# Graph layers with folded sums in three bf16 parts, and early expert rows: one kernel on one Trainium2 core

## The chip, the cores and the metric

The kernel runs on one core of one Trainium2 chip. The metric is the device time of one execution in microseconds (us); the median over the runs is what is compared.

## What is computed

The reference is a block of three parts over N = 3125 tokens of width D = 256 in fp32.

```
h = layernorm(x)                                   # no gain
ew = clip(|edge_weight|, 1e-6); deg = segment_sum(ew, dst) + 1; dis = 1/sqrt(deg)
for W, b, g, be in two layers:                     # 50,000 edges src -> dst, dst sorted
    xw = h @ W
    agg = segment_sum(dis[src]*ew*dis[dst] * xw[src], dst) + dis^2 * xw + b
    h = relu(layernorm(agg)*g + be) + h
x = x + h
# mixture of 16 experts, each token to its 2 best
n = layernorm(x); logits = n @ gate_w + gate_b; top 2, softmax of the two
y = n + sum_k w_k * (relu(n @ w1[e_k] + b1[e_k]) @ w2[e_k] + b2[e_k])
out = x + layernorm(y)*gamma + beta
```

The gate's bias has a spread of 0.388, the logits' own spread is 16 * 0.02 = 0.32. So the experts are loaded unevenly. Computed from the reference's own inputs, the 16 experts get 115, 28, 2028, 135, 1120, 1083, 7, 4, 57, 50, 8, 341, 741, 0, 532 and 1 of the 6250 assignments. Of the 18 token tiles that the kernel seats first (the tokens from 896 up), experts 0 to 3 get 87, 14, 1436 and 102.

## The kernel before, in words

Tokens lie in NT = 25 tiles of 128. A graph layer is a dense product: the edge weights are laid out as a matrix in DRAM (`weights_by_cell`), whose rows are not tokens but 128 x VT = 26 "virtual tiles" (v = dst + number of the block of 256 edges), so that rows which two blocks of edges write don't meet. The products of a virtual tile are its raw sums; a second small product, the fold, adds the raw rows of virtual tiles t, t+1 and t+2 that belong to a token tile.

Four stretches follow each other in time.

1. **Edges to matrix.** 196 blocks of 256 edges (`s`), in 98 pairs (`p`). For a pair a compare makes a 0/1 matrix of equal (src, dst) keys, on VectorE (`compare`, L656) or, for the 28 pairs of `ACT_PAIRS`, on ScalarE (`act_compare`, L907: four Abs, L916, and a Relu, L921); TensorE sums the equal edges' weights with it (`weigh`, L1074, in bf16). GpSimd then scatters the cells with 391 indirect DMAs (`place`, L474), chunk of 4 blocks by chunk, into the matrix that SyncE blanked tile by tile (L366). Beside it run the degrees, the first layernorm, and the tables h @ W1. GpSimd starts when `limits_ready` (VectorE's `limits_back`) says how many chunks each tile waits for. Constants come from GpSimd iotas (L437 to L459); `limits` waits for all 14 (`LATE_CONSTS`).
2. **Layer 1**, steps k = 0 to 25 of the loop at L1210 on, and
3. **Layer 2**, steps k = 26 to 51, tiles in falling order. In step k TensorE makes the raw sums of one virtual tile: 25 fp32 products of 128x128 by 128x256 (L1238), from a ring of three matrix tiles that SyncE loads (L386; in layer 1 each load first waits for the scatter's semaphores `seconds`, L381). Inside the step, after 4 of the 25 (`s == 4`), it folds the raw sums of step k-1 (`combine`, L1182): at most three products of `fold` (0/1, made by VectorE in `folding`, L756 and L759) by `ov`, ScalarE's fp32 copy of the raw sums (`take_out`, L962). The same step also turns a tile (L1096 or L1190) and makes its product or its gate logits (L1107, L1198). VectorE finishes the folded tile (`finish_tile`, L764 to L800: degree scale, bias, layernorm, relu, residual; ScalarE makes its NaN marks and roots, L966 to L975), and in layer 2 also finds slots for an earlier tile (`seat`, L827 to L832) and chooses the experts of another (`choose`, L807 to L821). GpSimd writes each seated tile's token numbers to their slots in DRAM (L522, `homes_in`). Between its ring loads SyncE issues the experts' weights: `load_up` (L142) and `load_down` (L147), 512 KB each. The last 17 of them stand at its end, after the waits for the steps that free their room.
4. **Experts.** The graph part is one block of the program and the experts' part the next; between them all five engines meet at a barrier, SyncE's issues included. Then VectorE makes the table of expert blocks (L1538 to L1557, 60 entries), SyncE loads the rows of slots (`load_ids`, L1377; the first `FIXED` = 4 blocks of 128 rows belong to experts 0 to 3 and need no table, but all slots written), GpSimd gathers the tokens of a block (`fetch`, L1333), and TensorE turns and multiplies them (L1401, L1418, L1430), block after block, 58 in the usual case. A last block (L1644 on) adds the two experts' rows of each token and normalises.

The fold and the order around it, which the change touches:

```
def combine(k):
    pe.wait_ge(fold_ready, k + 1)
    pe.wait_ge(ov_ready, k + 1)
...
for s in range(NT):
    if s == 4:
        combine(k - 1)
```

## Time and profile before

| what | value |
|---|---|
| median of 3 runs | 1240.26 us (1239.3 to 1245.99) |
| profiled execution, own time | 1235.6 us |
| its span | 1234.1 us |
| TensorE busy | 1095.5 us, 89% |
| VectorE busy | 708.5 us, 57% |
| GpSimd busy | 594.1 us, 48% |
| ScalarE busy | 386.6 us, 31% |

The span runs from the first to the last instruction. Edges to matrix take it to 259 us, layer 1 to 585 us, layer 2 to 935 us, the experts from 966 to 1195 us, the last block the rest. In rows of the trace a time is where an instruction starts, then how long it takes; an fp32 product shows as two MATMUL records. In brackets stands how long the engine sat idle before it, and whose result ended that.

### The profile page before, as it was taken

The page shows a single profiled execution, that of the slowest core. Times are in us where ns is not written, and L with a number is a line of the kernel's source. Part 1 is how long each engine was busy: PE and PEld are TensorE (multiplying, and loading weights), DVE is VectorE, ACT ScalarE, POOL GpSimd, SP SyncE. Part 2 cuts the span into 40 slices and gives each one's busy share as a digit, 9 for nine tenths or more (in the row PEclk, how much of TensorE's full clock was granted, in tenths as well). Part 3 has the DMA queues.
Part 4 walks back from the last instruction along what each step waited for, and adds up shares of the span by engine and source line. Part 5 has one row for each costly group of instructions (what it writes and reads, how often), then busy time and mean ns, then how long its engine had stood idle before and what let it go on. Part 6 is the DMA issues. An engine that isn't in the chain of part 4 may idle for free. (4 is left out here: it accounts for less than half of the span.)

```text
span 1234.1 us, 19478 instructions
## 1 busy us (share of the span) xinstructions
PE 1095.5 (89%) x6441; PEld 956.5 (78%) x6444; DVE 708.5 (57%) x2025; ACT 386.6 (31%) x879; POOL 594.1 (48%) x625
## 2 busy tenths in 40 slices
PE   2687687699999999999799999999993699999966
PEld 1566565588888888888588888888882699999955
DVE  8999743543434434434347777777777354555437
ACT  0578545831111111111111111111111133333357
POOL 4777777777777777750001111111112355555525
PEclk9999887999999999999799999999997799999989
DMA  7999540033433433430145535445447422222237
GB/s 283 294 392 385 221 161 2 2 114 107 149 119 107 151 117 107 150 118 1 51 150 188 207 129 194 163 147 181 145 168 248 130 74 70 74 71 74 69 100 248
DMA packets 79728, 180.76 MB, mean 146 GB/s; under 512 B 28994, under 2 KB 58316, under 8 KB 73228
## 3 DMA queue, kind: packets, MB, share of 16 engines
q1 hardware_dynamic: 48360, 151.67, 34.3%
q0 software_dynamic: 19776, 15.76, 4.8%
q10 hardware_dynamic: 11492, 12.07, 3.0%
q8 instruction: 54, 0.88, 0.3%
q14 instruction: 46, 0.38, 0.1%
HBM read 122.12 MB, written 57.33 MB: 145 GB/s over the span
## 5 line engine op out<-in xcount | busy, mean ns | idle before, releaser
L474 POOL DMA_INDIRECT weights_by_cell<-w_cell,cell x391 | 399.7, 1022 | 132.8 <-issue 118.0
L1238 PE MATMUL ps<-w 128*128 128x256 f32 x1300 | 300.7, 384 | 1.1 <-ACT w L904 1.1
L1238 PE MATMUL ps<-x_rows,w 128*128 128x256 f32 x1250 | 281.4, 379 | 0.3 <-DVE w_cell L662 0.3
L1238 PEld LDWEIGHTS ps<-w 128*128 128x128 f32 x1300 | 243.0, 191 | 33.0 <-ACT w L904 2.6
L1238 PEld LDWEIGHTS ps<-x_rows,w 128*128 128x128 f32 x1250 | 235.7, 190 | 31.5 <-DVE w_cell L662 0.4
L522 POOL DMA_INDIRECT token_and_home_of_slot<-pair,slot_id x50 | 49.6, 992 | 353.2 <-DVE slot_id L832 345.6
L1567 DVE TENSOR_SCALAR hidt<-ps,b1t 128x128 f32<-128x128 f32 x232 | 65.3, 344 | 90.9 <-PE ps L1418 90.9
L1430 PE MATMUL ps<-w,hidt 128*128 (+1 forms) x464 | 109.8, 379 | 0.0
L1418 PEld LDWEIGHTS ps<-xt,w1s 128*128 128x128 f32 x880 | 106.9, 192 | 2.8
L1046 PE MATMUL ps<-key_part,pick 128*128 128x256 f16 x196 | 50.4, 353 | 65.8 <-DVE layer L656 36.0
L1418 PE MATMUL ps<-xt,w1s 128*128 128x128 f32 x880 | 107.1, 275 | 0.0
L656 DVE TENSOR_TENSOR layer<-ps,w 128x1024 bf16<-128x1024 f32 x70 | 84.9, 1219 | 31.1 <-PE ps L1046 30.3
L1339 POOL DMA_INDIRECT expert_rows_by_token<-yb,ids x58 | 57.0, 983 | 91.4 <-DVE yb L1582 91.1
L1430 PEld LDWEIGHTS ps<-w,hidt 128*128 128x128 f32 x464 | 83.6, 190 | 9.0
L773 DVE COPY_PREDICATED layer<-mark,zeros 128x256 f32<-128x256 int32 x50 | 22.5, 450 | 108.2 <-ACT mark L966 108.2
L1046 PEld LDWEIGHTS ps<-key_part,pick 128*128 128x128 f16 x196 | 15.9, 112 | 80.2 <-DVE layer L656 38.7
L1333 POOL DMA_INDIRECT xb<-normalised_rows,ids x60 | 58.6, 976 | 31.3 <-PE ps L1401 16.0
L1182 PE MATMUL ps<-layer 128*128 128x256 f32 x296 | 72.4, 379 | 0.3 <-ACT layer L962 0.3
L764 DVE TENSOR_TENSOR layer<-ps,x_rows 128x256 f32<-128x256 f32 x25 | 10.6, 426 | 102.1 <-PE ps L1182 102.1
L1492 ACT ACTIVATE xt<-ps 128x256 f32<-128x256 f32 x60 | 23.0, 383 | 144.7 <-PE ps L1401 144.7
L1107 PE MATMUL ps<-wmat,ht 128*128 128x256 f32 x200 | 61.3, 435 | 5.8 <-ACT ht L895 5.6
L1081 PE MATMUL ps<-w,hot 128*128 128x75 bf16 x400 | 64.8, 319 | 0.0
(242 smaller groups left out, 1470.0 us busy)
## 6 DMA issues: line engine op xcount, KB each, us to landing
w<-weights_by_cell SPq DMA_DIRECT2D x49, 1600.0 KB, 7.2
weights_by_cell<-w SPq DMA_DIRECT2D x26, 1600.0 KB, 8.7
w<-in_L_ffn_w_dram SPq DMA_DIRECT2D x32, 512.0 KB, 8.6
weights_by_cell<-w_cell,cell POOLq DMA_INDIRECT x391
w<-in_x_dram ACTq DMA_DIRECT2D x1, 3072.0 KB
hot<-in_x_dram ACTq DMA_DIRECT2D x24, 128.0 KB, 2.1
normalised_rows<-hot ACTq DMA_DIRECT2D x24, 128.0 KB, 4.8
out_dram<-w SPq DMA_DIRECT2D x24, 128.0 KB
```

The costliest lines, as they stand in the source:

```text
L474: pool.indirect_dma_start(adj[:, :], bass.IndirectOffsetOnAxis(ap=cell[0:m, c:c + 1].bitcast(U32), axis=0), w_cell[0:m, n, half * CH + j:h ...
L656: dve.tensor_tensor(same[:, d % MRING, :, :, :], bank(d % KBANKS).rearrange("p (s h q) -> p s h q", s=2, h=1).to_broadcast(wide), own.rear ...
L1046: mm = pe.matmul(bank(at, k * SBE, (k + 1) * SBE), pick[:, j:j + 1].to_broadcast([P, P]), key_part[:, g, :], start=True, stop=True)
L1081: mm = pe.matmul(bank(6, 0, 3 * NT), hot[:, i % DRING, :, k], hot_w[:, i % DRING, :, :, k].rearrange("p a b -> p (a b)"), start=(i == 0 an ...
L1107: mm = pe.matmul(bank(6 if q else 3, 0, D), ht[:, i % 2, c, :], wmat[:, q, c, :], start=(c == 0), stop=(c == KD - 1))
L1182: mm = pe.matmul(bank(2 + i % 3, 0, D), fold[:, k % 2, (d - lo) * P:(d - lo + 1) * P], ov[:, k % 2, :], start=begins, stop=ends)
L1238: mm = pe.matmul(bank(k % 2, 0, D), ring[:, place_of(k), s * P:(s + 1) * P], tab[q][:, s, :], start=(s == 0), stop=(s == NT - 1))
L1333: pool.indirect_dma_start(xb[:, b % ring, :], None, x2_dram[0:N, :], bass.IndirectOffsetOnAxis(ap=ids[:, b % IDS, 0:1].bitcast(U32), axis= ...
L1339: pool.indirect_dma_start(planes[:, :], bass.IndirectOffsetOnAxis(ap=ids[:, b % IDS, 1:2].bitcast(U32), axis=0), yb[:, b % 2, :], None).th ...
L1418: mm = pe.matmul(ph[s][:, f * P:(f + 1) * P], w, xt[:, s, c, :], start=(c == 0), stop=(c == KD - 1))
L1430: mm = pe.matmul(py[s], hidt[:, s, c, :], w, start=(c == 0), stop=(c == KF - 1))
L1567: ins = dve.tensor_scalar(hidt[:, s, c, :], ph[s][:, c * P:(c + 1) * P], bias, 0.0, ALU.add, ALU.max)
```

## The change

- **Fold in bf16, both layers** (`SPLIT_LAYERS` = 2). The raw sums are cut in three bf16 parts whose sum is exact: ScalarE copies the high part, VectorE subtracts it from the sums (`split`), ScalarE copies the middle part of the rest, VectorE subtracts again. `combine` makes three bf16 products per tile with a bf16 `fold` where it made one in fp32. It stands after 7 of the 25 products of the step instead of 4.
- **First expert rows.** In SyncE's queue, before the wait for step 50 and the 17 last weight loads, stand now: a wait for `need_ready`, which VectorE's `seat(18)` sets, a wait for the slots of the first 18 tiles (`homes_first`), a wait for `homes_in` up to a number held in a register, and the four loads of `ids`. The number is 16 (one more scatter), plus 208 if the smallest count of experts 0 to 3 over the first 18 tiles is under 128; 224 is all of the other 7 tiles. The rows b1 are loaded in the first stretch by SyncE.
- **ScalarE compares ahead.** `act_compare` of the next pair of `ACT_PAIRS` stands after ScalarE's work of the pair before, no more right ahead of its use.
- **Small ones.** `limits` waits for 8 constants; the big iotas are cut in pieces of 256 or 512 elements; x is loaded after the first blank and the other blanks after x; the table of empty slots (`unplaced`) has room of its own, so ScalarE no longer waits for its store (L936 before); a few semaphores are merged.

```diff
+SEATED = 18
+PARTS, SPLIT_LAYERS = 3, 2
...
                         sp.wait_ge(blanked[t % 2], 16 * (t // 2 + t % 2))
+                    if t == 1:
+                        sp.wait_ge(x_in, 32)
                     if t == 3:
...
+                        sp.dma_start(b1r[TURN * KF:EXPERTS * KF, :],
+                                     g["eb1"][0:EXPERTS - TURN].rearrange("e (c p) -> (e c) p", p=P)).then_inc(b_in, 16)
+                        sp.dma_start(b1r[0:TURN * KF, :],
+                                     g["eb1"][EXPERTS - TURN:EXPERTS].rearrange("e (c p) -> (e c) p", p=P)).then_inc(b_in, 16)
...
                 sp.wait_ge(ov_ps, 2 * VT - 2)
                 for e in (3, 4):
                     load_up(sp, e)
+                later = sp.alloc_register("later_need")
+                sp.wait_ge(need_ready, 1)
+                sp.reg_load(later, later_need[0:1, 0:1])
+                sp.wait_ge(homes_first, 32 * SEATED)
+                sp.wait_ge(homes_in, sp.snap(later, min_val=16, max_val=32 * (NT - SEATED)))
+                for b in range(FIXED):
+                    sp.dma_start(ids[:, b, :], home[b * REGION:b * REGION + P, :]).then_inc(ids_in[b], 16)
                 sp.wait_ge(ov_ps, 2 * VT - 1)
                 for e in range(3):
...
-                pool.iota(low, pattern=[[1, NT * P + 1]], base=0, channel_multiplier=0,
-                          allow_small_or_imprecise_dtypes=True).then_inc(late_consts, 1)
+                for k in range(0, NT * P + 1, 512):
+                    pool.iota(low[:, k:min(k + 512, NT * P + 1)], pattern=[[1, min(512, NT * P + 1 - k)]], base=k, channel_multiplier=0,
+                              allow_small_or_imprecise_dtypes=True).then_inc(late_consts, 1)
...
                             home[:, :], bass.IndirectOffsetOnAxis(ap=slot_id[0:m, k, d:d + 1].bitcast(U32), axis=0),
-                            pair[0:m, k, d, :], None).then_inc(homes_in, 16)
+                            pair[0:m, k, d, :], None).then_inc(homes_first if r < SEATED else homes_in, 16)
...
-                    dve.wait_ge(late_consts, LATE_CONSTS)
+                    dve.wait_ge(late_consts, LIMIT_CONSTS)
...
+                    dve.tensor_tensor((fold_bits if in_parts(k) else fold)[:, k % 2, 0:w], reach[:, 0:w], reach[:, 1:w + 1], ALU.subtract).then_inc(fold_ready, 1)
+
+                def split(k):
+
+                    dve.wait_ge(ov_high, k + 1)
+                    dve.tensor_tensor(ov_rest, ov_bank(k), ov_parts[:, k % 2, 0, :], ALU.subtract).then_inc(ov_left, 1)
+                    dve.wait_ge(ov_left, k + 1)
+                    dve.wait_ge(ov_mid, k + 1)
+                    dve.tensor_tensor(ov_parts[:, k % 2, 2, :], ov_rest, ov_parts[:, k % 2, 1, :], ALU.subtract).then_inc(ov_ready, 1)
 
...
+                    if r == SEATED:
+                        link(dve.tensor_copy(rank0[:, :], bank(5, 0, FIXED)))
                     dve.tensor_tensor(rank[:, :], bank(5, 0, EXPERTS), base[:, :], ALU.add).then_inc(rank_read, 1)
                     dve.wait_ge(rank_read, r + 1)
+                    if r == SEATED:
+                        link(dve.tensor_reduce(fewest[:, :], rank0[:, :], AX_X, ALU.min))
+                        link(dve.tensor_scalar(fewest[:, :], fewest[:, :], float(P), 32.0 * (NT - SEATED) - 16, ALU.is_lt, ALU.mult))
+                        dve.tensor_scalar(later_need[:, :], fewest[:, :], 16.0, None, ALU.add).then_inc(need_ready, 1)
...
                     nxt = k + 1 if k + 1 < 2 * VT else None
+                    if in_parts(k):
+                        split(k)
                     if not done_at(q, t):
...
-                    if s % 2 == 0 and by_act(s // 2):
-                        act_compare(s // 2)
+                    if s == 2 * ACT_PAIRS[0] - 5:
+                        act_compare(ACT_PAIRS[0])
+                    if s % 2 == 1 and by_act(s // 2) and s // 2 != ACT_PAIRS[-1]:
+                        act_compare(ACT_PAIRS[ACT_PAIRS.index(s // 2) + 1])
...
-                        if t == 0:
-                            act.wait_ge(unplaced_out, 16)
...
-                    act.activation(ov[:, k % 2, :], bank(k % 2 if k else 6, 0, D), ACT.Copy).then_inc(ov_ready, 1)
+                    if in_parts(k):
+                        act.activation(ov_parts[:, k % 2, 0, :], ov_bank(k), ACT.Copy).then_inc(ov_high, 1)
+                        act.wait_ge(ov_left, k + 1)
+                        act.activation(ov_parts[:, k % 2, 1, :], ov_rest, ACT.Copy).then_inc(ov_mid, 1)
+                    else:
+                        act.activation(ov[:, k % 2, :], ov_bank(k), ACT.Copy).then_inc(ov_ready, 1)
...
-                        mm = pe.matmul(bank(2 + i % 3, 0, D), fold[:, k % 2, (d - lo) * P:(d - lo + 1) * P], ov[:, k % 2, :],
-                                       start=begins, stop=ends)
+                        cols = slice((d - lo) * P, (d - lo + 1) * P)
+                        if in_parts(k):
+                            for c in range(PARTS):
+                                mm = pe.matmul(bank(2 + i % 3, 0, D), fold_bits[:, k % 2, cols], ov_parts[:, k % 2, c, :],
+                                               start=begins and c == 0, stop=ends and c == PARTS - 1)
+                        else:
+                            mm = pe.matmul(bank(2 + i % 3, 0, D), fold[:, k % 2, cols], ov[:, k % 2, :], start=begins, stop=ends)
                     mm.then_inc(combined, 1)
...
-                        if s == 4:
+                        if s == (7 if in_parts(k - 1) else 4):
                             combine(k - 1)
...
-                    sp.wait_ge(homes_in, 32 * NT)
+                    sp.wait_ge(homes_in, 32 * (NT - SEATED))
```

VectorE in a steady step of layer 2 (ps is PSUM, layer the work rows; `seat` is L827 to L832, `choose` L807 to L821, the next tile's finish begins at L764). Before:

```order
L832 CAST slot_id<-which 128x2 [waits vector_chain]
L807 TENSOR_TENSOR logit<-ps,gbias 128x16 [waits logit_ps,slot_ready]
L817 TENSOR_TENSOR both<-one 128x16 [waits vector_chain]
L821 TENSOR_TENSOR before<-before,both 128x16 [waits rank_ps,chosen]
L764 TENSOR_TENSOR layer<-ps,w 128x256 [waits folded,vector_chain]
```

With the change:

```order
L881 CAST slot_id<-which 128x2 [waits vector_chain]
L850 TENSOR_TENSOR logit<-ps,gbias 128x16 [waits logit_ps,slot_ready]
L860 TENSOR_TENSOR both<-one 128x16 [waits vector_chain]
L864 TENSOR_TENSOR before<-before,both 128x16 [waits rank_ps,chosen]
L799 TENSOR_TENSOR layer<-ps,layer 128x256 [waits ov_high,vector_chain]
L802 TENSOR_TENSOR layer<-layer 128x256 [waits ov_mid,ov_left]
L807 TENSOR_TENSOR layer<-ps,w 128x256 [waits folded]
```

The two subtractions of `split` stand between the end of one tile and the wait for the fold of the next.

TensorE in the same place (L1182, in the change L1242, is the fold; L1190/L1252 turns a tile for the gate; L1205, L1206 and L1267, L1268 count slots). Before:

```order
L1238 MATMUL ps<-w 128x256 [waits ov_ready,loaded0]
L1238 MATMUL ps<-w 128x256 x3
L1182 MATMUL ps<-layer 128x256 [waits agg_read,ov_ready,fold_ready]
L1182 MATMUL ps<-layer 128x256 x2
L1238 MATMUL ps<-w 128x256 x2
L1205 MATMUL ps<-both,below 128x16 [waits rank_read,chosen]
L1206 MATMUL ps<-before,ones 128x16
L1238 MATMUL ps<-w 128x256 x2
L1190 MATMUL ps<-ident,hot 128x128 [waits x2t_ready,x2_ready]
```

With the change:

```order
L1300 MATMUL ps<-w 128x256 [waits ov_ready,loaded0]
L1300 MATMUL ps<-w 128x256 x5
L1267 MATMUL ps<-both,below 128x16 [waits rank_read,chosen]
L1268 MATMUL ps<-before,ones 128x16
L1300 MATMUL ps<-w 128x256
L1242 MATMUL ps<-layer 128x256 [waits agg_read,ov_ready,fold_ready]
L1242 MATMUL ps<-layer 128x256 x8
L1300 MATMUL ps<-w 128x256
L1252 MATMUL ps<-ident,hot 128x128 [waits x2t_ready,x2_ready]
```

The fold waits for `ov_ready` as before, which VectorE's second subtraction now gives, and one product stands between it and the turn, where four stood.

SyncE's queue at the end of the graph part (L142/L146 are `load_up`, L147/L151 `load_down`). Before:

```order
L142 DMA w<-in_L_ffn_w_dram 128x2x512 [waits ov_ps]
L142 DMA w<-in_L_ffn_w_dram 128x2x512 x2
L142 DMA w<-in_L_ffn_w_dram 128x2x512 [waits agg_read,ov_ps]
L142 DMA w<-in_L_ffn_w_dram 128x2x512 x9
L142 DMA w<-in_L_ffn_w_dram 128x2x512 [waits z_ready,fold_ready]
L147 DMA w<-in_L_ffn_w_dram 128x4x256 x3
L330 UNCONDITIONAL_BRANCH [waits small_in]
L1360 UNCONDITIONAL_BRANCH [waits barrier_Pool_Activation_PE_DVE_SP_release]
L1377 DMA ids<-token_and_home_of_slot 128x2 [waits homes_in]
L1377 DMA ids<-token_and_home_of_slot 128x2 x3
```

With the change:

```order
L428 TENSOR_LOAD later_need [waits need_ready]
L432 DMA ids<-token_and_home_of_slot 128x2 [waits homes_first,homes_in]
L432 DMA ids<-token_and_home_of_slot 128x2 x3
L146 DMA w<-in_L_ffn_w_dram 128x2x512 [waits ov_ps]
L146 DMA w<-in_L_ffn_w_dram 128x2x512 x2
L146 DMA w<-in_L_ffn_w_dram 128x2x512 [waits agg_read,ov_ps]
L146 DMA w<-in_L_ffn_w_dram 128x2x512 x9
L146 DMA w<-in_L_ffn_w_dram 128x2x512 [waits z_ready,fold_ready]
L151 DMA w<-in_L_ffn_w_dram 128x4x256 x3
L350 UNCONDITIONAL_BRANCH [waits small_in]
L1420 UNCONDITIONAL_BRANCH [waits barrier_Pool_Activation_PE_DVE_SP_release]
```

The wait for `homes_in` moved from behind the barrier to ahead of the 17 loads and of the barrier.

## Rows read from the trace of the kernel before

**Rows 1.** Busy times by stretch: stretch, PE, PEld, DVE, ACT, POOL, PEclk, DMA share, GB/s
```profile
262.00:597.00 335.00, 334.81 (x1574) 293.88 (x1572) 130.07 (x313) 58.16 (x143) 217.20 (x223) 1.00 0.33 113
...
600.00:630.00 30.00, 25.39 (x94) 20.30 (x95) 5.54 (x14) 3.68 (x9) 0.00 (x0) 0.77 0.30 107
...
612.00:932.00 320.00, 320.00 (x1576) 280.58 (x1575) 221.12 (x738) 56.49 (x144) 41.81 (x42) 1.00 0.48 167
```

**Rows 2.** Timeline of VectorE, one steady step of layer 2
```profile
755.70 0.42 DVE L764 TENSOR_TENSOR layer<-ps,w 128x256 f32<-128x256 f32 x1 [0.53 <-PE ps L1182]
...
758.71 0.45 DVE L773 COPY_PREDICATED layer<-mark,zeros 128x256 f32<-128x256 int32 x1 [1.14 <-ACT mark L966]
...
767.89 0.17 DVE L821 TENSOR_TENSOR before<-before,both 128x16 bf16<-128x16 bf16 x1
768.59 0.43 DVE L764 TENSOR_TENSOR layer<-ps,w 128x256 f32<-128x256 f32 x1 [0.54 <-PE ps L1182]
```

**Rows 3.** Timeline of TensorE, the same step
```profile
754.14 1.46 PE L1182 MATMUL ps<-layer 128*128 128x256 f32 x6
755.43 1.03 PE L1238 MATMUL ps<-w 128*128 128x256 f32 x4
...
757.29 0.38 PE L1190 MATMUL ps<-ident,hot 128*128 128x128 f32 x2
```

**Rows 4.** Timeline of VectorE at layer 2's first tile, and line L764 over layer 2
```profile
627.66 0.42 DVE L764 TENSOR_TENSOR layer<-ps,w 128x256 f32<-128x256 f32 x1 [23.59 <-PE ps L1182]
...
629.45 0.45 DVE L773 COPY_PREDICATED layer<-mark,zeros 128x256 f32<-128x256 int32 x1
...
L764 DVE TENSOR_TENSOR layer<-ps,w x25: 425/426/427, 627.7 to 935.2; 128x256 f32<-128x256 f32 x25
```

**Rows 5.** Timeline of ScalarE, one copy of raw sums
```profile
765.50 0.38 ACT L962 ACTIVATE layer<-ps 128x256 f32<-128x256 f32 x1 [1.00 <-PE ps L1238]
```

**Rows 6.** Timeline of TensorE near 257 us: 16-bit products at the full clock
```profile
256.91 0.38 PE L1046 MATMUL ps<-key_part,pick 128*128 128x256 f16 x2
...
257.75 0.35 PE L1074 MATMUL ps<-w,layer 128*128 128x3 bf16 x8
```

**Rows 7.** Waits up to 270 us: us in total, times, longest
```profile
PE ps L1046 <- ACT layer L921: 29.6, 12, 4.9
```

**Rows 8.** Timelines of TensorE, SyncE's queue and GpSimd, end of layer 1
```profile
573.32 1.46 PE L1182 MATMUL ps<-layer 128*128 128x256 f32 x6
...
584.77 1.89 PE L1238 MATMUL ps<-w 128*128 128x256 f32 x8
...
540.67 7.92 SPq L386 DMA_DIRECT2D w<-weights_by_cell  x2
...
542.38 0.96 POOL L474 DMA_INDIRECT weights_by_cell<-w_cell,cell  x1 [0.30 <-issue]
```

**Rows 9.** Timeline of VectorE, the same operation beside a GpSimd iota and alone
```profile
4.75 1.93 DVE L565 TENSOR_SCALAR w<-w 128x128 int32<-128x128 f32 x1
...
28.87 0.22 DVE L565 TENSOR_SCALAR w<-w 128x128 int32<-128x128 f32 x1
```

**Rows 10.** SyncE's queue and landings (L522, slots) at the end of layer 2
```profile
932.64 1.43 SPq L142 DMA_DIRECT2D w<-in_L_ffn_w_dram  x3
...
946.49 3.05 SPq L147 DMA_DIRECT2D w<-in_L_ffn_w_dram  x1
...
DMA to landing us min/median/max: 4.2/6.5/9.0
```

**Rows 11.** Timelines of GpSimd, ScalarE's queue, VectorE and TensorE at the barrier
```profile
951.01 0.97 POOL L522 DMA_INDIRECT token_and_home_of_slot<-pair,slot_id  x1 [0.30 <-issue]
...
963.49 1.00 POOL L1333 DMA_INDIRECT xb<-normalised_rows,ids  x1 [11.15 <-DMA ids<-token_and_home_of_slot]
...
950.40 0.34 ACTq L1473 DMA_DIRECT2D b1r<-in_L_ffn_b_dram  x1
...
966.51 0.66 PE L1401 MATMUL ps<-ident,xb 128*128 128x128 f32 x2 [9.36 <-DMA xb<-normalised_rows,ids]
```

More of the change, by code:

```diff
@@ L131, in program @@
         totals = keep("totals", [P, EXPERTS], I32)
+        ids = keep("ids", [P, IDS, 2], I32)
+        b1r = keep("b1r", [EXPERTS * KF, P])
         w1 = keep("w1", [P, EXPERTS * KD * F])
@@ L148, in load_down @@
                          ew2[e].rearrange("(k p) f -> p k f", p=P)).then_inc(w_in[e // WGROUP], 16)
+        homes_first, b_in = sem("homes_first"), sem("b_in")
+        ids_in = [sem(f"ids_in{k}") for k in range(IDS)]
         homes_in, x2_out = sem("homes_in"), [sem(f"x2_out{k}") for k in range(XRING)]
@@ L161, in gnn @@
     best, homes_in, x2_out, load_up, load_down = (g[n] for n in ("best", "homes_in", "x2_out", "load_up", "load_down"))
+    homes_first, b_in, ids, ids_in, b1r = (g[n] for n in ("homes_first", "b_in", "ids", "ids_in", "b1r"))
     x1_rows = first_rows = g["x1_rows"]
@@ L265, in gnn @@
         which = sb("which", [P, 2])
+        rank0 = sb("rank0", [P, FIXED])
+        fewest = sb("fewest", [P, 1])
+        later_need = sb("later_need", [P, 1], U16)
         one = sb("one", [P, 2, 2, EXPERTS])
@@ L452, in _ @@
                           allow_small_or_imprecise_dtypes=True).then_inc(late_consts, 1)
-                pool.iota(lo_ref, pattern=[[1, P], [0, DG]], base=0, channel_multiplier=0,
-                          allow_small_or_imprecise_dtypes=True).then_inc(late_consts, 1)
+                for k in range(0, P, P // 4):
+                    pool.iota(lo_ref[:, k:k + P // 4, :], pattern=[[1, P // 4], [0, DG]], base=k, channel_multiplier=0,
+                              allow_small_or_imprecise_dtypes=True).then_inc(late_consts, 1)
                 pool.iota(hi_ref[:, :, :], pattern=[[1, NT], [0, DG]], base=0, channel_multiplier=0,
@@ L1259, in experts @@
     homes_in, x2_out = g["homes_in"], g["x2_out"]
+    b_in, ids, ids_in, b1r = (g[n] for n in ("b_in", "ids", "ids_in", "b1r"))
     ps_slot, ps_a, ps_b, ps_c, ps_d = g["ps_slot"], g["ps_a"], g["ps_b"], g["ps_c"], g["ps_d"]
@@ L1285, in experts @@
             yb = sbi("yb", [P, 2, D])
-            ids = sbi("ids", [P, IDS, 2], I32)
             bnum = sbi("bnum", [P, DYN])
@@ L1306, in diag @@
                 return own_diag[:, at, k, :] if at < OWN_DIAGS else lent[:, at - OWN_DIAGS, k, :]
-            b_in, b2_in, b2_rest, counts, tv, table_ready, gap_ready, exp_ready = (
-                sem(n) for n in ("b_in", "b2_in", "b2_rest", "counts", "table_chain", "table_ready", "gap_ready", "exp_ready"))
-            ids_in = [sem(f"ids_in{k}") for k in range(IDS)]
+            b2_in, b2_rest, counts, tv, table_ready, gap_ready, exp_ready = (
+                sem(n) for n in ("b2_in", "b2_rest", "counts", "table_chain", "table_ready", "gap_ready", "exp_ready"))
             b1_ps, b1_ready = sem("b1_ps"), sem("b1_ready")
@@ L1361, in _ @@
                 def _(sp):
-                    sp.wait_ge(homes_in, 32 * NT)
+                    sp.wait_ge(homes_in, 32 * (NT - SEATED))
                     regs = [sp.alloc_register(f"row_tile{k}") for k in range(2)]
                     def load_ids(b):
-                        if b == FIXED:
-                            sp.wait_ge(table_ready, 1)
-                        if b >= FIXED:
-                            sp.reg_load(regs[b % 2], row_tile[0:1, b - FIXED:b - FIXED + 1])
+                        sp.reg_load(regs[b % 2], row_tile[0:1, b - FIXED:b - FIXED + 1])
                         if b >= IDS:
                             sp.wait_ge(y_out[b % 2], 16 * ((b - IDS) // 2 + 1))
-                        if b < FIXED:
-                            rows = home[b * REGION:b * REGION + P, :]
-                        else:
-                            at = sp.snap(regs[b % 2], min_val=0, max_val=ROWTILES - 1)
-                            rows = home[bass.ds(at * P, P), :]
-                        sp.dma_start(ids[:, b % IDS, :], rows).then_inc(ids_in[b % IDS], 16)
-                    for b in range(usual + 2):
+                        at = sp.snap(regs[b % 2], min_val=0, max_val=ROWTILES - 1)
+                        sp.dma_start(ids[:, b % IDS, :], home[bass.ds(at * P, P), :]).then_inc(ids_in[b % IDS], 16)
+                    sp.wait_ge(table_ready, 1)
+                    for b in range(FIXED, usual + 2):
                         load_ids(b)
```

75 lines of the change are left out of this document (40 added, 35 removed).

## The prediction, made before the changed kernel ran

> **What bounds the kernel now.** I read the busy times by stretch first, to see which engine is full where. From 262 to 597 us TensorE is busy 334.81 of 335.00 us, and from 612 to 932 us 320.00 of 320.00, at full clock: both layers are bound by TensorE. But in layer 2 VectorE is busy 221 of its 320 us in a chain of short dependent operations, so I look there for a second bound [rows 1]. Between the layers (600 to 630 us) the granted clock is 0.77: it falls when TensorE idles.
>
> Second, the timelines of one steady step of layer 2. VectorE starts a tile (L764) at 755.70 and the next at 768.59: 12.89 us per step. It waits twice inside: 1.14 us for ScalarE's mark and 0.54 us for the fold [rows 2]. Without the latter its chain is 12.35 us. So VectorE is half a microsecond from being the bound. The fold (six records, three fp32 products) takes 1.46 us: 6 x 0.213 and a tail of 0.18 [rows 3]. ScalarE copies a tile's sums in 0.38 us [rows 5].
>
> Third, the waits up to 270 us. TensorE waits 29.6 us in 12 pieces for ScalarE's compare [rows 7]. Fourth, the end of layer 1: GpSimd still scatters at 542.38, and SyncE's load of a matrix tile sits from 540.67 for 7.92 us in its queue behind the scatter [rows 8]. Fifth, the stretch between layer 2 and the experts: 14 weight loads leave SyncE's queue from 932.64 to 949.54, ScalarE's first issue behind the barrier is at 950.40, the last slots are scattered at 951.01 and land some 6.5 us later, GpSimd gathers the first expert rows at 963.49 after 11.15 us of idling for `ids`, and TensorE turns them at 966.51 [rows 10, 11].
>
> **The change part by part.**
>
> *First stretch.* ScalarE's compare ahead takes away most of the 29.6 us of waits; I hold 20 of it and the wait for the empty slots' table, some 8 more, recoverable for TensorE. But the end of layer 1 is not set by TensorE alone. Its last tiles need the scatter, which is GpSimd's: one after another, 391 of them at 0.96 us and 0.30 of issue [rows 8], about 1.3. The gain of the first stretch becomes idling of TensorE ahead of steps 22 to 24. What counts is how much earlier GpSimd starts. An operation that VectorE does beside the big iotas takes 1.93 us against 0.22 alone [rows 9]; cutting the iotas frees some such operations ahead of the limits, and two or three constants less are awaited. I take 1.5 us, between 0 and 3. Then the matrix tile of step 24 is asked for at 540.67 - 1.5 = 539.2 and lands some 7.2 us later (an estimate, inside the 4.2 to 9.0 us of the slots' landings [rows 10]), at 546.4. Two steps of 12.9 us and a little for a clock that drops while TensorE idles (2.2 us, from the 0.77 of rows 1) end layer 1 at 574.3, against 584.77: **-10.5** (-8 to -13).
>
> *Between the layers.* The fold of layer 1's last steps stands three products later: 3 x 0.43 = +1.28, with folds that are shorter by 0.7: **+0.5**. In layer 1 the shorter folds are inside the GpSimd bound and cost or give nothing more.
>
> *Price of a fold.* 16-bit products: eight loads of weights with three columns each take 0.35 us, two of 256 columns 0.38 [rows 6]. So I take a pass of 256 columns at 0.107 us (256 at 2.4 GHz), half of a record's 0.213, and weight loads run beside it. Nine passes are 9 x 0.107 + 0.18 = 1.14 us instead of 1.46: -0.32 per step for TensorE, to 12.57. By the Trainium skill (page "TensorE: Matmul & The Clock Gate", section "LDWEIGHTS (loading the stationary operand)") a load costs its number of columns divided by 1.2 in ns, 107 ns for 128; if none of the nine hid, the fold would take 1.9 to 2.1 us and layer 2 some 21 us more than I forecast. The eight loads in 0.35 us speak against that, so the sum goes by the row.
>
> *Layer 2, where VectorE closes a loop.* The split stands on VectorE between the end of one tile and the wait for the fold of the next. Before, the fold needed ScalarE's copy alone, and was nearly done when VectorE came. Now the fold of the next tile can't begin before VectorE has ended this one. Nothing hides it. The loop is:
> - from L764 to L773 with no wait, as at layer 2's first tile: 629.45 - 627.66 = 1.79 us [rows 4]. (In the steady step it is 3.01 with the mark's 1.14 in it. That wait should go, since one product instead of four stands between fold and turn, so ScalarE copies sooner.)
> - from 758.71 to the end of L821 at 768.06: 9.35 us [rows 2]
> - split: subtraction 0.43, copy 0.38 to 0.39, subtraction 0.42, two hand-overs of 0.04: 1.31 us (two-operand fp32 work of 128x256 is 0.42 us in rows 2, ScalarE's copy 0.38 in rows 5)
> - TensorE starts the fold behind the product in hand, 0.15 (0 to 0.43); fold 1.14; hand-over to L764 0.10.
>
> Together 13.84 us (13.5 to 14.2) against TensorE's own 12.57: the step is VectorE's, and TensorE idles 1.3 us in each. The 25 tiles' L764 lie from 627.7 to 935.2 [rows 4], 307.6 us for 24 intervals. With the change: two at 12.4 before `seat` and `choose` are in, 22 at 13.84 = 304.5, in all 329.3, less 0.2: **+21.5** (17 to 30; the low end is a fold hidden in the product's rest, the high end the mark's wait staying in).
>
> *The barrier.* Experts 0 to 3 have 87, 14, 1436 and 102 rows in the first 18 tiles. The smallest is under 128, so the register gets 224: all slots. SyncE then waits for the last slot scatter ahead of its 17 loads, and all engines meet only when those are issued. Taking layer 2 as ending when it did: the scatter of 951.01 lands 6.5 us later, 957.5 [rows 10, 11]. Four loads of `ids` at 0.48 (1.43 for 3) end at 959.4. Fourteen loads took 16.9 us, 1.21 each, while DMA was full (the last 3.05); 17 take 20.5: 979.9. The barrier opens 0.9 later at 980.8 instead of 950.4. `ids` is long there, so GpSimd fetches at 981.5, and TensorE turns 3.0 us later (963.49 to 966.51), plus 2 for rows that queue behind weight loads in flight: 986.5 against 966.51, **+20.0**. From below: 17 issues at the unthrottled 0.48 are 8.1 us, which gives +5.6; from above: landing 6.5 instead of 3.0 + 2, +21.5. VectorE's table of blocks starts 30 us later too, but ends near the time that its first entry is needed.
>
> *At nothing.* b1 in the first stretch (it was not what TensorE waited for last), x a little later (ScalarE's sums have slack), merged semaphores.
>
> Sum: -10.5 + 0.5 + 21.5 + 20.0 = **+31.5 us**. The profiled execution has 1235.6 us (span 1234.1), which gives 1267.1; the median shown is 1240.26, so I forecast **1272 us**.
>
> **Rivals.**
> - *Not slower, split hidden.* ScalarE and TensorE may swing in so that VectorE's two subtractions fall in its waits (0.54 + 1.14 = 1.68 us per step, over the 1.31 of the split). For it: the sum of the waits. Against: the 0.54 comes after the split's place. It decides when VectorE reaches L764 within 12.57 us. Then layer 2 gains 23 x 0.32 = 7.3 us: -10.5 + 0.5 - 7.3 + 20.0 = +2.7, **1243**. Chance 0.08.
> - *Not slower, first rows early.* The register's wait doesn't hold all slots (the smallest count is 128 or more on the chip), so `ids` is there at the old barrier: TensorE turns at 955.6, -10.9: sum +0.6, **1241**. Against: the counts. Chance 0.08.
> - *Both*, the faster side: -10.5 + 0.5 - 7.3 - 10.9 = -28.2, **1212**. Chance 0.04.
> - *GpSimd is not the bound*: the 28 us of the first stretch come through, 17.5 more than taken: +14, **1254**. Against: the scatter runs until 543 in any case. Chance 0.06.
> - *As forecast*: 0.74.
>
> **How the numbers follow.** Low ends of the forecast's own terms (-13, 0, +17, +5.6) make +10, high ends (-8, +2, +30, +21.5) +46, both hardly at once; its own range is 1254 to 1286. To hold 8 in 10 the range reaches down to the two cases near 1242: **1241 to 1286**. Half a per cent, 6 us, is about what a measurement of this kernel can tell from no change. Faster: 0.04, the third rival. Same: the first two, 0.16. Slower: 0.80.
>
> **What the profile after would show.** Right: in layer 2 L764's (now L807) interval is 13.8, TensorE idles about 1.3 us ahead of each fold, released by VectorE's second subtraction; `ids` is issued after the last slot scatter, the 17 loads behind it, and GpSimd's first gather is over 15 us later after the end of layer 2 than before. The waits for ScalarE's compare are gone, and TensorE waits for matrix tiles before steps 22 to 24. Wrong: a step of 12.6 with full TensorE in layer 2; a barrier within a few microseconds of the last fold; a first layer that ends at 585 or at 560.

## The result, and the profile after

The changed kernel takes 1262.18 us (median of 4 runs, 1261.92 to 1262.93), the one before 1241.03 us in its runs beside it (1239.3 to 1245.99). The ratio is 1.0172, with a 95% interval of 1.014 to 1.0204: 21 us slower. The forecast was 1272 in a range of 1241 to 1286, slower: right in direction, and 10 us too long.

| from the traces, us | before | after | difference | forecast |
|---|---|---|---|---|
| last tile of layer 1 (start of L764, now L807) | 597.3 | 584.1 | -13.2 | -10.5 |
| from there to layer 2's first tile | 30.4 | 32.0 | +1.6 | +0.5 |
| layer 2, first to last tile | 307.6 | 329.6 | +22.0 | +21.5 |
| last tile to TensorE's first turn of the experts | 31.3 | 47.1 | +15.8 | +20.0 |
| from there to the end of the span | 267.6 | 267.3 | -0.3 | 0 |
| span | 1234.1 | 1260.1 | +26.0 | +31.5 |

Busy times by stretch, the same as [rows 1]:

```profile
262.00:597.00 335.00, 309.60 (x1505) 265.69 (x1503) 146.30 (x356) 68.34 (x168) 212.14 (x225) 0.95 0.29 99
600.00:630.00 30.00, 30.00 (x147) 25.98 (x146) 12.09 (x31) 4.04 (x10) 0.00 (x0) 0.95 0.50 186
612.00:932.00 320.00, 298.84 (x1554) 251.34 (x1553) 233.90 (x772) 64.52 (x162) 41.84 (x42) 1.00 0.45 156
```

TensorE, full before in both layers, now lacks 25.4 us in the first window and 21.2 in the third. Of the 25.4, 18.3 are waits for matrix tiles; the other 7 lie behind layer 1's last tile, since the window reaches 13 us past it now. The reasons in the two layers differ.

**Layer 2.** VectorE in a steady step, to set against [rows 2]:

```profile
776.60 0.17 DVE L864 TENSOR_TENSOR before<-before,both 128x16 bf16<-128x16 bf16 x1
776.80 0.42 DVE L799 TENSOR_TENSOR layer<-ps,layer 128x256 f32<-128x256 f32 x1
777.77 0.43 DVE L802 TENSOR_TENSOR layer<-layer 128x256 bf16<-128x256 f32 x1 [0.55 <-ACT layer L1017]
779.48 0.43 DVE L807 TENSOR_TENSOR layer<-ps,w 128x256 f32<-128x256 f32 x1 [1.28 <-PE ps L1242]
...
781.27 0.44 DVE L816 COPY_PREDICATED layer<-mark,zeros 128x256 f32<-128x256 int32 x1
```

TensorE in the same step, to set against [rows 3]:

```profile
764.46 1.14 PE L1242 MATMUL ps<-layer 128*128 128x256 bf16 x9 [0.94 <-issue]
...
776.68 0.68 PE L1300 MATMUL ps<-w 128*128 128x256 f32 x2
778.30 1.14 PE L1242 MATMUL ps<-layer 128*128 128x256 bf16 x9 [0.94 <-issue]
779.28 0.60 PE L1300 MATMUL ps<-w 128*128 128x256 f32 x2
...
792.16 1.14 PE L1242 MATMUL ps<-layer 128*128 128x256 bf16 x9 [0.94 <-issue]
```

Read them together. L864 ends the old tile, the split follows (L799, 0.55 us of waiting for ScalarE's middle copy, L802), L802 ends at 778.20, TensorE starts the fold at 778.30, and L807 starts the next tile behind it after 1.28 us. The profile calls TensorE's 0.94 us before the fold "issue"; the end of L802 shows that it is the split. The wait for the mark at L816 (1.14 us at L773 before) is gone. The fold of nine passes takes 1.14 us. Folds start at 764.46, 778.30 and 792.16: the steps are 13.84 and 13.86 us.

**Layer 1.** Ahead of its last steps TensorE now waits for matrix tiles (timelines of SyncE's queue and TensorE, then the waits of 262 to 545 us and of the first 270; last, the first operation of each tile of layer 1, after and before, and the scatters):

```profile
537.30 7.04 SPq L411 DMA_DIRECT2D w<-weights_by_cell  x2
...
543.99 5.29 PE L1300 MATMUL ps<-x_rows,w 128*128 128x256 f32 x14 [6.01 <-DMA w<-weights_by_cell]
...
571.82 3.19 PE L1300 MATMUL ps<-w 128*128 128x256 f32 x14
...
PE ps L1300 <- DMA w<-weights_by_cell: 18.3, 4, 7.1
...
PE ps L1103 <- ACT layer L973: 3.6, 5, 1.9
...
L807 DVE TENSOR_TENSOR layer<-ps,x_rows x25: 418/426/427, 254.7 to 584.1; 128x256 f32<-128x256 f32 x25
L764 DVE TENSOR_TENSOR layer<-ps,x_rows x25: 419/426/427, 286.1 to 597.3; 128x256 f32<-128x256 f32 x25
L508 POOL DMA_INDIRECT weights_by_cell<-w_cell,cell x391: 911/967/3557, 20.3 to 537.8; - x196
```

The waits for ScalarE's compare fell from 29.6 us [rows 7] to 3.6, and layer 1's first tile starts at 254.7 instead of 286.1; 18.3 us of that are given back as four waits for matrix tiles, whose loads wait for the scatter. GpSimd's first scatter is at 20.28 instead of 23.47, its last at 537.8 instead of 542.38.

**Barrier.** SyncE's queue, GpSimd and TensorE, for [rows 10, 11]:

```profile
964.01 1.76 SPq L432 DMA_DIRECT2D ids<-token_and_home_of_slot  x4
965.82 11.75 SPq L146 DMA_DIRECT2D w<-in_L_ffn_w_dram  x14
977.62 6.98 SPq L151 DMA_DIRECT2D w<-in_L_ffn_w_dram  x3
...
961.49 0.97 POOL L556 DMA_INDIRECT token_and_home_of_slot<-pair,slot_id  x1 [0.30 <-issue]
986.08 1.00 POOL L1393 DMA_INDIRECT xb<-normalised_rows,ids  x1 [0.60 <-issue]
...
985.19 0.34 PE L1447 MATMUL ps<-ident,b1r 64*128 64x64 f32 x1 [24.99 <-PEq L350]
992.84 0.66 PE L1455 MATMUL ps<-ident,xb 128*128 128x128 f32 x2 [7.31 <-DMA xb<-normalised_rows,ids]
```

The four ids go out 1.55 us after the last slot scatter ended, and the 17 loads (issued in 18.8 us) only behind them. TensorE stands 25.0 us at the barrier, GpSimd 22.7. After it, the rows that GpSimd asks for at 986.08 are there for TensorE at 992.84, 6.8 us later, against 3.0 before. The DMA engines are full in that stretch (share 1.07, against 0.27 before), which fits rows that queue behind the weight loads; no run tests it.

### The profile page after: what moved, and what is told of

The parts are those of the page before. It is cut to its first block and busy times, and to the rows that moved or that the text cites. A ratio compares the mean times of both kernels' runs of the same rounds, so it can differ in the third digit from the quotient of the medians.

```text
span 1260.1 us, 19997 instructions
## 1 busy us (share of the span) xinstructions
PE 1087.1 (86%) x6589; PEld 936.6 (74%) x6592; DVE 747.0 (59%) x2133; ACT 407.2 (32%) x931; POOL 589.8 (47%) x634
## 5 line engine op out<-in xcount | busy, mean ns | idle before, releaser
L508 POOL DMA_INDIRECT weights_by_cell<-w_cell,cell x391 | 393.7, 1007 | 133.2 <-issue 124.6
L1300 PE MATMUL ps<-x_rows,w 128*128 128x256 f32 x1250 | 289.7, 386 | 18.6 <-DMA w<-weights_by_cell 18.3
L1300 PEld LDWEIGHTS ps<-x_rows,w 128*128 128x128 f32 x1250 | 238.5, 194 | 52.3 <-DMA w<-weights_by_cell 19.9
L1242 PE MATMUL ps<-layer 128*128 128x256 bf16 x444 | 57.2, 273 | 24.0 <-issue 19.0
L1242 PEld LDWEIGHTS ps<-layer 128*128 128x128 bf16 x444 | 41.9, 98 | 40.5 <-issue 32.4
L1164 PE MATMUL ps<-wmat,ht 128*128 128x256 f32 x200 | 55.5, 402 | 5.8 <-ACT ht L947 5.6
L1538 ACT ACTIVATE w1s<-w 128x1024 f32 x56 | 59.2, 1058 | 2.7 <-issue 0.5
L1131 PEld LDWEIGHTS ps<-w,layer 128*128 128x128 bf16 x784 | 47.0, 106 | 15.1 <-issue 0.8
```

What stands on the lines that cost most here:

```text
L508: pool.indirect_dma_start(adj[:, :], bass.IndirectOffsetOnAxis(ap=cell[0:m, c:c + 1].bitcast(U32), axis=0), w_cell[0:m, n, half * CH + j:h ...
L1164: mm = pe.matmul(bank(6 if q else 3, 0, D), ht[:, i % 2, c, :], wmat[:, q, c, :], start=(c == 0), stop=(c == KD - 1))
L1242: mm = pe.matmul(bank(2 + i % 3, 0, D), fold_bits[:, k % 2, cols], ov_parts[:, k % 2, c, :], start=begins and c == 0, stop=ends and c == P ...
L1300: mm = pe.matmul(bank(k % 2, 0, D), ring[:, place_of(k), s * P:(s + 1) * P], tab[q][:, s, :], start=(s == 0), stop=(s == NT - 1))
L1538: act.activation(w1s[:, k, :, :].rearrange("p c f -> p (c f)"), w1[:, bass.ds(e * (KD * F), KD * F)], ACT.Copy).then_inc(w1_ready, 1)
```

## The experiments

The runs were made in groups, each with the kernel before beside it. In two groups, the one that timed the change and one later, the kernel before takes 1241 and 1242 us: the *short* groups. In three others it takes 1573, 1572 and 1571 us, since there the first stretch is drawn out: the *long* groups. Why isn't known. The record has the same chip number, 8, for two of the long groups and for the later short one, and 12 for the third long one, so it isn't told by the chip.

Two kernels, those of experiments 6 and 8, were traced in both kinds of group. Their layer 2 takes 301.4 us in both, and 307.6 and 307.5; from its last tile to the end it is 297.0 (long) and 295.5, and 296.5 (long) and 296.7. So of runs in long groups I read the stages behind layer 1, and compare times only with the kernel before in the same group. Layer 1 can't be read there: with the change its tiles lie within 302.8 us, 12.6 a step, since it starts so late that the scatter is no longer met.

The changed kernel itself was not run in a long group. Its stages there are seen in the runs that leave them as they are: layer 2 takes 329.6 us in experiment 2, and from the last tile to the first turn it is 47.3 us in both runs of experiment 7, against 329.6 and 47.1 in its own trace.

**1. Layer 2 in fp32 again** (long group).

```diff
-PARTS, SPLIT_LAYERS = 3, 2
+PARTS, SPLIT_LAYERS = 3, 1
```

> The changed kernel with layer 2 folded in fp32 as before, after 4 of 25 products; layer 1 keeps the three bf16 parts. Theory (VectorE's split closes layer 2's loop): the step goes from 13.85 back to 12.89 us, first to last tile of layer 2 from 329.6 to some 307.6, the time falls by 22 us to about 1240. Rival (layer 2's loss is in its overlap with loads, not in the split): the step stays above 13.4 and the time above 1254.

Measured: 1587.09 us, 1.0084 (1.0056 to 1.0113) of the kernel before. Layer 2's tiles lie from 967.9 to 1275.5: 307.6 us, exactly as before. So the 22 us of layer 2 come with the bf16 fold. Three things are undone here at once, the split on VectorE, the nine passes and the fold's place after 7 of the 25; experiments 4 and 5 tell them apart. The time expected can't be compared, since the changed kernel has no time in this group.

**2. The ids behind the barrier again** (two long groups): the seven lines in SyncE's queue go, and the experts' part issues the four loads first.

```diff
-                later = sp.alloc_register("later_need")
...
-                sp.wait_ge(homes_first, 32 * SEATED)
-                sp.wait_ge(homes_in, sp.snap(later, min_val=16, max_val=32 * (NT - SEATED)))
-                for b in range(FIXED):
-                    sp.dma_start(ids[:, b, :], home[b * REGION:b * REGION + P, :]).then_inc(ids_in[b], 16)
...
+                    sp.wait_ge(g["homes_first"], 32 * SEATED)
                     sp.wait_ge(homes_in, 32 * (NT - SEATED))
+                    for b in range(FIXED):
+                        sp.dma_start(ids[:, b, :], home[b * REGION:b * REGION + P, :]).then_inc(ids_in[b], 16)
```

> The changed kernel with the wait for the slots and the four ids loads moved back behind the barrier. Theory (the wait holds 17 loads and the barrier): from the last tile of layer 2 to TensorE's first turn of the experts 31.3 us as before instead of 47.1, so the time falls by 15.8 to about 1246. Rival (the experts then wait for their weights or the table, and it is given back): the first turn is early but the time falls by less than 8, above 1254.

> ids behind the barrier once more, where the kernel before takes 1241. From layer 2's last tile to the end 296.9 us instead of 314.4, as in its first run: 1262.2 - 17.5 = 1244.7. Rival (given back later): above 1254.

Measured: 1591.0 us, 1.0121 (1.005 to 1.0191), and 1590.21 us, 1.0139 (1.0072 to 1.0206). Layer 2's tiles and TensorE's first turn in the first run:

```profile
L800 DVE TENSOR_TENSOR layer<-ps,w x25: 425/426/427, 957.6 to 1287.2; 128x256 f32<-128x256 f32 x25
...
L1451 PE MATMUL ps<-ident,xb x120: 272/273/475, 1316.2 to 1537.3; 128*128 128x128 f32 x120
```

From layer 2's last tile to the first turn it is 1316.2 - 1287.2 = 29.0 us, and 28.5 in the second run, instead of 47.1; to the end of the span 296.9 and 296.3 instead of 314.4. The 17.5 us are not given back. Over all traces, the stretch from the last tile to the end takes 295.5 to 300.2 us in the eight with the ids behind the barrier (298.9 in the kernel before) and 314.4 to 317.3 in the six with the ids ahead of it. So single traces differ by some us in this stretch, and the loss is clear of that. This kernel was not timed in a short group.

**3. Both undone** (long group).

> Both undone: layer 2 in fp32 and the ids behind the barrier. Theory: the two terms add, -22 and -15.8, so 1224. Rival (they hide each other, since weight loads wait for layer 2's steps too): the sum is less than 30, above 1232.

Measured: 1573.17 us, 0.9999 (0.9966 to 1.0033). Layer 2 takes 307.5 us, its last tile to the end 300.2. The two terms add, but for some 3 us, no more than the eight traces above differ by.

**4. The split ahead of `seat` and `choose`** (long group).

```diff
                         nxt = None
+                        if q == 1 and k + 1 < 2 * VT and in_parts(k + 1):
+                            split(k + 1)
                         if r == 1:
```

(and no split at the head of the next pass of the loop).

> The changed kernel with layer 2's split put ahead of seat and choose on VectorE instead of behind them; nothing else. Theory (the place of the split closes the loop, nine bf16 passes are cheap): the step falls from 13.85 to 12.6 to 12.8 us, bound by TensorE again, the time by 23 to 28 us to about 1236. Rival (the nine passes and their weight loads, or VectorE's total work, bind): the step stays at 13.3 or more, the time above 1250.

Measured: 1621.13 us, 1.0313 (1.024 to 1.0387). The step is 14.4 us and layer 2's tiles take 345.6: slower than the 329.6 with the split behind. The rival's bound (13.3 or more) holds, but a step above 13.85 came out of neither theory. TensorE's timeline shows what it waits for:

```profile
1099.71 7.72 PE L1302 MATMUL ps<-w 128*128 128x256 f32 x35
1109.21 0.18 PE L1269 MATMUL ps<-both,below 128*128 128x16 bf16 x1 [1.77 <-DVE both L860]
1109.24 0.17 PE L1270 MATMUL ps<-before,ones 128*128 128x16 bf16 x1
1109.27 0.68 PE L1302 MATMUL ps<-w 128*128 128x256 f32 x2
1109.79 1.15 PE L1244 MATMUL ps<-layer 128*128 128x256 bf16 x9
```

VectorE in the same step:

```profile
1106.34 0.42 DVE L802 TENSOR_TENSOR layer<-layer 128x256 bf16<-128x256 f32 x1 [0.55 <-ACT layer L1019]
...
1108.97 0.17 DVE L860 TENSOR_TENSOR both<-one 128x16 bf16<-128x16 f32 x1
...
1111.04 0.42 DVE L807 TENSOR_TENSOR layer<-ps,w 128x256 f32<-128x256 f32 x1 [1.69 <-PE ps L1244]
```

The three parts are ready at 1106.76, 3 us before the fold. But the counting products (L1269), which stand after 6 of the 25, wait for L860 in `choose`, and the fold stands behind them in TensorE's order since the change moved it from 4 to 7. VectorE's next tile waits for the fold: a second loop. From 1000 to 1200 us TensorE waits 24.9 us in 14 pieces for L860; in the changed kernel, from 640 to 900 us, 0.5 us in 2. So this loop was hidden behind the first as long as the split came last.

**5. The same, and the counting products after 10 of the 25** (long group).

```diff
-                        if k >= VT + 4 and s == 6:
+                        if k >= VT + 4 and s == 10:
                             count(k - VT - 4)
```

> The early split again, and TensorE's two counting products moved from after 6 to after 10 of the 25 products, behind the fold. Theory (in the run before, the loop closed through the counting products, which wait for choose and stood ahead of the fold): the step falls to 12.6 to 12.8 us, from layer 2's first to its last tile some 304 us instead of 329.6 (345.6 with the early split alone), and nothing holds TensorE ahead of the fold. Rival (VectorE's work in the step is by itself more than TensorE's): the step stays at 13.2 or more, above 317 us.

Measured: 1582.6 us, 1.0068 (1.0046 to 1.0091). Line L807 over layer 2, in the change, in experiment 1, 4 and 5:

```profile
L807 DVE TENSOR_TENSOR layer<-ps,w x25: 425/426/426, 616.1 to 945.7; 128x256 f32<-128x256 f32 x25
```

```profile
L807 DVE TENSOR_TENSOR layer<-ps,w x25: 425/426/428, 967.9 to 1275.5; 128x256 f32<-128x256 f32 x25
```

```profile
L807 DVE TENSOR_TENSOR layer<-ps,w x25: 425/426/429, 954.6 to 1300.2; 128x256 f32<-128x256 f32 x25
```

```profile
L807 DVE TENSOR_TENSOR layer<-ps,w x25: 425/425/427, 966.6 to 1268.0; 128x256 f32<-128x256 f32 x25
```

329.6, 307.6, 345.6 and 301.4 us. TensorE's folds of this run are 12.58 us apart, with no idle time ahead of them:

```profile
1102.82 1.15 PE L1244 MATMUL ps<-layer 128*128 128x256 bf16 x9
...
1115.40 1.15 PE L1244 MATMUL ps<-layer 128*128 128x256 bf16 x9
```

That is the 12.57 that the forecast worked out as TensorE's own. So nine bf16 passes with nine weight loads cost the 1.14 to 1.15 us that the forecast had from [rows 3] and [rows 6], with the fold still after 7 of the 25. The loss was in the order alone: where the split stands, and what stands ahead of the fold. Of the 28 us gained in layer 2 this run gives some 3 back, with 317.3 us from the last tile to the end; with the ids behind the barrier as well, in experiment 6, that isn't seen.

**6. That, and the ids behind the barrier** (long group, then a short one).

> The same with the ids behind the barrier as well. Theory: layer 2 in some 304 us and from its last tile to the end some 297 to 299 us instead of 314.4, together 40 us below the changed kernel and 18 to 22 below the one before, a ratio of 0.983 to 0.987 to it. Rival (the faster layer 2 collides with its weight loads, or the experts wait): less than 10 us below the one before.

> The early split, late counting products and ids behind the barrier once more, to have its time where the first stretch isn't drawn out. If the kernel before takes 1241 here: layer 2's tiles in 301.4 us, from its last tile to the end 297, the changed kernel's first stretch, so 1262.2 - 28.2 - 17.4 = 1216.6 us, a ratio of 0.980. If the stages don't add, above 1226.

Measured: in the long group 1565.51 us, 0.9968 (0.9946 to 0.999); layer 2 301.4 us, from its last tile to the end 297.0. Both stages are as expected, but the time is some 6 us below the kernel before instead of 18 to 22. What the change gained in layer 1 seems to be missing there, as in experiment 8; no trace of the kernel before in a long group shows it. In the short group **1216.9 us** (1215.06 to 1219.29) beside 1241.76, a ratio of 0.9799 (0.976 to 0.9839): 45 us below the changed kernel (timed in the other short group), 25 below the one before, and 0.3 from the sum of the stages. So close a hit has some luck in it: by the spans of the traces it gains 46.9 us on the changed kernel, not 45. This version beats both.

**7. x in the place where it was** (two long groups): ScalarE's wait for the first blank goes, and SyncE waits for x ahead of blank 3 again.

> The changed kernel with x loaded as before (no wait for the first blank, the blanks 1 and 2 not behind it). Theory A (the order of x and the blanks started the scatter earlier): GpSimd's first scatter goes from 20.3 back to about 23.5 us, the last from 537.8 to about 541, the time rises by some 3 to 5 us. Theory B, my forecast's (the iotas in pieces did): the first scatter stays at 20.3 and the time within 1 us.

> x loaded as in the kernel before, once more, where the kernel before takes 1241. Theory A (the order of x and the blanks started the scatter earlier): first scatter 23 to 23.5 us, last 541, layer 1's last tile 587 to 588 instead of 584.1, time 1265 to 1267. Theory B (the cut iotas did, or it makes no difference): last tile within 1 us of 584.1, time 1262.

Measured: 1602.93 us, 1.0192 (1.016 to 1.0223), and 1608.29 us, 1.0238 (1.0178 to 1.0297). The first scatter is at 22.1 and 21.5 us; in the other runs of the changed order it lies at 19.3 to 20.7, in the three traces of the old kernel or its variant at 23.4 to 23.6. So neither theory holds alone; both causes have a share. The traces tell them apart. VectorE's last operation for the limits (L646, now L680) starts at 20.1 or 20.2 us in the old kernel and its variant, and at 17.0 to 18.4 in all traces of the changed one, with either order of x. These 2 to 3 us belong to the cut iotas and the fewer awaited constants, which were not tested apart. From there to the first scatter it is 2.3 us in all nine traces with the new order of x and 3.6 or 3.7 in the two with the old one: 1.3 us for the order. (In the old kernel and its variant it is 3.2 to 3.5.) The effect on layer 1's end can't be read in the long groups, where layer 1's last tile varies by 17 us over the runs of the changed kernel and its variants (925.3 to 941.9).

**8. ScalarE's compare ahead, alone, in the kernel before** (long group, then a short one).

```diff
-                    if s % 2 == 0 and by_act(s // 2):
-                        act_compare(s // 2)
+                    if s == 2 * ACT_PAIRS[0] - 5:
+                        act_compare(ACT_PAIRS[0])
+                    if s % 2 == 1 and by_act(s // 2) and s // 2 != ACT_PAIRS[-1]:
+                        act_compare(ACT_PAIRS[ACT_PAIRS.index(s // 2) + 1])
```

> The kernel before with ScalarE's compare ahead, alone. Theory (GpSimd's scatter sets the end of layer 1): the waits for ScalarE's compare fall from 29.6 us to under 5, layer 1 starts up to 20 us earlier, but its last tile stays within 2 us of where it was and the time within 0.3% of the kernel before. Rival (TensorE sets it): the time falls by 15 to 20 us.

> ScalarE's compare ahead alone in the kernel before, once more for the same reason. Theory: layer 1 starts up to 20 us earlier, its last tile stays within 2 us of 597.3, the time within 0.3%. Rival: the time falls by 15 to 20 us.

Measured: in the long group 1570.6 us, 0.9993 (0.9964 to 1.0021). In the short one **1226.93 us** (1226.54 to 1227.48), 0.9875 (0.9837 to 0.9914), 15 us faster: the theory as I wrote it fell. Line L764 over layer 1, the waits up to 270 us and TensorE in layer 1's last steps, in the short group:

```profile
L764 DVE TENSOR_TENSOR layer<-ps,x_rows x25: 420/426/427, 262.4 to 589.9; 128x256 f32<-128x256 f32 x25
...
PE ps L1048 <- ACT layer L921: 6.9, 6, 3.3
...
548.69 3.78 PE L1240 MATMUL ps<-x_rows,w 128*128 128x256 f32 x8 [4.87 <-DMA w<-weights_by_cell]
```

Layer 1 starts 23.7 us earlier (262.4 for 286.1) and ends 7.4 earlier (589.9 for 597.3). Before, TensorE was full to the end of layer 1 and bound it [rows 1]; the scatter alone would have let it end 7.4 us earlier. With the compares ahead TensorE reaches the scatter and waits. So TensorE set the end before, GpSimd sets it now, and the first 7.4 us of a gain come through. The distance from the last scatter to layer 1's last tile says the same: 46.6 us here (589.9 - 543.3), 46.3 in the change, 45.9 in experiment 6 in the short group, but 54.9 in the kernel before.

The spans differ by 9.1 us, the medians by 15, so the rival's 15 to 20 is met by the medians alone. Of the 9.1, 7.4 are layer 1's, -0.5 lies between the layers, and 2.2 behind layer 2, where this edit changes nothing.

## Why the prediction was right, and where it was off

**Direction and mechanisms.** Both losses were where the sum put them. In layer 2 the split closed the loop through VectorE: forecast 13.84 us for the step, measured 13.84 and 13.86, undone by experiment 1. (Of the 1.3 us that TensorE was to lose in each step the rows show 0.94 as idle; against experiment 5 the steps are longer by the full 1.27.) At the barrier the ids went out only behind the last slot scatter, as they must with 224, all slots, in the register, and SyncE's 17 loads stood behind the wait, undone by experiment 2. The two rivals near 1242 and the one at 1212 fell with them. The rival of the hidden split put 7.3 us of gain on layer 2; experiment 5, where the split is hidden, has 6.2. The rival that GpSimd is not the bound was at 1254; the 18.3 us of waits for matrix tiles speak against it.

**Layer 1: right path, one term too small.** The forecast had TensorE as the bound of layer 1 before and the scatter close behind. Its numbers leave the scatter 9.0 us of room (the 10.5 less the 1.5 by which it was to start earlier); experiment 8 measured 7.4. It then counted from the scatter, and that part held. The matrix tile was there at 543.99 us and not at 546.4, the two steps behind it took 27.8 us against some 28.0, and the product that stood at 584.77 stands at 571.82. That is -12.9 of the -13.2.

So the term that was mis-sized is how much earlier the scatter comes. The forecast had 1.5 us. It was 3.2 at the first scatter, some 1.3 of it by the order of x, which I had costed at nothing, and 4.6 at the last; against experiment 8, whose last scatter is at 543.3, even 5.5. Why it grows on the way isn't known.

Layer 1's first tile is 31.4 us earlier, of which experiment 8 has 23.7. The forecast had given the wait for the empty slots' table some 8; that would be the rest, but no run tests it.

**Between the layers: +1.6 instead of +0.5.** Over all 14 traces this stretch takes 28.5 to 32.1 us, so one trace of each kernel can't tell the two numbers apart.

**Barrier: +15.8 instead of +20.0.** Three terms of it were too long and one too short: the slots' landing after the last scatter (taken 6.5 us from its start; the ids went out 2.5 us after it, with the DMA engines at a share of 0.01 from 962 to 964 us), the 17 issues (20.5; 18.8), the opening (0.9; about 0.6), and the first rows (3.0 + 2; 6.8 from gather to turn, with the DMA engines full).

**The total.** +26.0 us in the traces against a sum of +31.5. The rest of the miss is the reference point: the profiled execution of the kernel before had 1235.6 us, 5.4 below its median of 1241.0, and the changed kernel's runs spread over 1 us only. The sum was put on the median as it stood. Small slips in the forecast's sums change little: the 0.2 taken off layer 2's 329.3 has no reason given, and the barrier's low end of +5.6 also drops the 2 us for queued rows, with which it is +7.6. By traces, 1235.6 + 26 = 1261.6, which is the changed kernel's median within 0.6. Experiment 8 has the same gap, 9.1 us by spans and 15 by medians, but it rests on the same trace of the kernel before. The 4 runs of the changed kernel spread over 1.0 us and those of experiment 8 over 0.9, the 7 of the kernel before in the later short group over 9.0. It fits that TensorE's waits of the first stretch vary from run to run and reach the end only where TensorE bounds layer 1. But experiment 6, where the scatter bounds layer 1 too, spreads over 4.2 us, and no trace of a slower run of the kernel before shows it, so this stays open. The mean granted clock doesn't explain it: of those 7 runs the longest, 1248.03 us, has the highest, 0.964.

## What to carry to other kernels

Before work is put between two engines that are within half a microsecond of each other, follow the loop: what must the second engine have ended before the first may start, and what stands ahead of it in either queue. The same work placed where its inputs are ready, with the products that wait for the late engine moved behind it, turned a loss of 22 us in layer 2 into a gain of 6. A wait put into a queue to start four small loads early holds all that stands behind it, here 17 large loads and a barrier, for 16 to 18 us. And a sum that is made on one profiled execution should say how far that execution lies from the median.

## What the runs showed of the hardware

- In the long groups TensorE waits long in the first stretch for nothing that the profile names, and the longest waits of VectorE and ScalarE are put down to "remote". Experiment 1: waits of 60 to 600 us (L1131 are the weighing products), then one row of TensorE's timeline:

```profile
DVE hot L719 <- remote: 147.4, 14, 22.7
ACT w L968 <- remote: 133.2, 7, 37.2
...
PE ps L1131 <- issue: 65.5, 49, 2.6
...
250.56 0.30 PE L1138 MATMUL ps<-w,hot 128*128 128x75 bf16 x1 [2.51 <-issue]
```

  The last scatter comes at 605 to 617 us instead of 538 to 543, and the kernel takes 1572 us instead of 1241. Layer 2 takes the same time in both kinds of group (301.4 us for experiment 6 in either), and from its last tile to the end the same within 1.5 us. The cause is not settled, and by the chip numbers on record it isn't one chip against another.
- Nine bf16 passes of 256 columns with a weight load of 128 columns each take 1.14 to 1.15 us, and the step with them 12.58. The loads lie beside the products: in experiment 5 the nine loads take 1.08 us from 1102.61 on, the nine passes 1.15 us from 1102.82 on. The loads of the folds in the change:

```profile
L1242 PEld LDWEIGHTS ps<-layer 128*128 128x128 bf16 x444 | 41.9, 98 | 40.5 <-issue 32.4
```

  By the Trainium skill ("TensorE: Matmul & The Clock Gate", "LDWEIGHTS (loading the stationary operand)") a load costs its number of columns divided by 1.2 in ns, which makes 107 ns for 128; the trace has 98 in the mean. Unhidden, such loads would have added some 21 us to layer 2, by the prediction's estimate; experiment 5 shows them hidden.
- With the DMA engines all but idle the four ids went out 2.5 us after the last slot scatter had started. Where the ids stand behind the barrier and weight loads keep the DMA engines busy (shares of 0.86 to 1.07 around them), they went out 6.4 us (experiment 6, short group) and 7.4 us (experiment 2, first run) after it, and in the kernel before the slot scatters landed 6.5 us after their start in the median [rows 10].
